# A gather of weight rows in two halves, each with its own signal, in a sparse mixture-of-experts kernel on one core

## What is computed

```python
rates = relu(x) * 0.001
c = cond[:, None, :] + cumsum(rates, axis=1)
spikes = (floor(c) - floor(c one step earlier)) / 0.001      # mostly zero
probs = softmax(spikes @ router_w.T);  top 2, gates normalized to sum 1
keep = position of the token within its expert < C           # C = 640
h = gelu(einsum('ech,ehf->ecf', expert_in, w1))              # w1: 8 x 256 x 1024
y = einsum('ecf,efh->ech', h, w2)                            # w2: 8 x 1024 x 256
out = x + sum over the two experts of gate * y
```

## Time and profile before

| | us |
|---|---|
| median of 3 runs | 68.56 |
| lowest and highest run | 67.09, 68.94 |
| the profiled execution's own time | 67.18 |
| its span, first to last instruction | 65.5 |
| TensorE busy within the span (PE) | 53.0 |
| VectorE (DVE), ScalarE (ACT), GpSimd (POOL) busy | 36.2, 25.9, 18.2 |

### The profile page before, as it was taken

One profiled execution on the slowest core, in us unless ns is written; L12 is line 12 of the kernel. 1 busy time (PEld: TensorE's weight loads), 2 busy tenths in 40 slices (PEclk: granted clock), 3 DMA queues, 4 the chain that ended last, 5 costly groups with the idle time before them and its releaser, 6 DMA issues.

```text
span 65.5 us, 1291 instructions
## 1 busy us (share of the span) xinstructions
PE 53.0 (81%) x435; PEld 32.7 (50%) x435; DVE 36.2 (55%) x165; ACT 25.9 (39%) x60; POOL 18.2 (28%) x55
## 2 busy tenths in 40 slices
PE   3985999999679971199979999999999999994000
PEld 1312434554345661144539668986597666661000
DVE  0377097877799677988668924867061022026000
ACT  0599425756770039409996300681027002000000
POOL 6799943000002500306668810000000000000740
PEclk9999999999999998555599999999999999999985
DMA  0499999999999999700487860698899991000030
GB/s 0 119 362 320 353 329 355 370 336 344 345 349 348 351 350 343 219 13 0 105 190 228 326 234 35 134 357 283 264 381 384 382 358 35 0 0 0 15 126 10
DMA packets 13545, 14.82 MB, mean 226 GB/s; under 512 B 652, under 2 KB 13046, under 8 KB 13536
## 3 DMA queue, kind: packets, MB, share of 16 engines
q1 hardware_dynamic: 12608, 12.62, 59.4%
q0 software_dynamic: 816, 2.01, 9.9%
q10 hardware_dynamic: 112, 0.07, 0.5%
HBM read 13.08 MB, written 2.36 MB: 236 GB/s over the span
## 4 chain that ended last, share of the span: by engine, by line
PE 63%; ACT 8%; DVE 7%; DMA 7%; issue 5%; POOL 3%; ACTq 2%; POOLq 0%; DVEq 0%
PE bank L662 22%; PE bank L646 12%; PE bank L501 11%; DMA w_got<-in_L_ffn_w_dram,w_index 7%; PE bank L552 6%; POOL out_dram L476 3%; ACT w_got L753 3%; PE bank L507 3%; PE bank L518 2%; PE bank L678 2%; ACT L753 2%; ACTq L749 1%; PE bank L567 1%; PE bank L679 1%; ACT limit L790 1%
## 5 line engine op out<-in xcount | busy, mean ns | idle before, releaser
L662 PE MATMUL bank<-w_sb,spare_sb 128*64 128x256 f32 x128 | 14.7, 382 | 0.0
L662 PEld LDWEIGHTS bank<-w_sb,spare_sb 128*64 128x64 f32 x128 | 8.8, 137 | 4.5
L488 PE MATMUL bank<-ones_b 128*128 128x512 bf16 x23 | 9.4, 555 | 1.1 <-POOL ones_b L380 1.1
L501 PE MATMUL bank<-rate,cum_seq 128*128 128x512 f32 x16 | 8.4, 604 | 0.1
L476 POOL DMA_INDIRECT out_dram<-floors,out_index x2 | 2.0, 1020 | 22.9 <-DVE floors L1092 22.6
L646 PE MATMUL bank<-ev_pair,w_got 128*128 128x128 f32 x64 | 7.8, 278 | 0.4 <-DMA w_got<-in_L_ffn_w_dram,w_index 0.4
L770 ACT ACTIVATE spikes<-bank 128x256 bf16<-128x256 f32 x16 | 6.0, 381 | 5.3 <-PE bank L518 5.2
L646 PEld LDWEIGHTS bank<-ev_pair,w_got 128*128 128x128 f32 x64 | 7.4, 192 | 0.9 <-DMA w_got<-in_L_ffn_w_dram,w_index 0.9
L902 DVE TENSOR_SCALAR floors<-bank 128x512 bf16<-128x512 f32 x8 | 5.5, 691 | 3.5 <-PE bank L507 3.2
L783 ACT ACTIVATE spare_sb<-bank 128x512 f32<-128x512 f32 x8 | 4.8, 597 | 6.7 <-PE bank L646 6.6
L996 DVE TENSOR_SCALAR rate<-bank,pair_gate 128x256 f32<-128x256 f32 x4 | 1.9, 484 | 9.2 <-PE bank L662 9.2
(11 more groups left out here) (176 smaller groups left out, 79.2 us busy)
## 6 DMA issues: line engine op xcount, KB each, us to landing
w_sb<-in_L_ffn_w_dram SPq DMA_DIRECT2D x8, 1024.0 KB, 11.3
x_sb<-in_x_dram SPq DMA_DIRECT2D x8, 256.0 KB, 4.1
out_dram<-x_sb SPq DMA_DIRECT2D x1, 2048.0 KB, 13.7
cond<-in_cond_dram ACTq DMA_DIRECT2D x2, 32.0 KB, 2.3
w_got<-in_L_ffn_w_dram,w_index POOLq DMA_INDIRECT x4, 5.8
cond<-in_cond_dram SPq DMA_DIRECT2D x1, 32.0 KB, 1.9
x_rows<-in_x_dram,out_index POOLq DMA_INDIRECT x2, 3.7
out_dram<-floors,out_index POOLq DMA_INDIRECT x2, 2.8
```

What stands on the lines that cost most here:

```text
L488: nc.tensor.matmul(bank[2][:, 0:4 * P], ones_b[:, :], ones_b[:, :].unsqueeze(1).to_broadcast([P, 4, P]), start=True, stop=True)
L501: nc.tensor.matmul(CUM[g % 4][:, 0:GW], cum_seq[:, :], rate[:, g % RING, :, :].rearrange("p j c -> p (j c)"), start=True, stop=False)
L662: mm = nc.tensor.matmul(Y[d % 2][at, :], hT[:, d % 2, f, at], w2_sb[:, 2 * d + side, f, :], start=(f == 0), stop=(f == FC - 1))
```

## The change

`gather(0)` issues two indexed DMAs instead of one: the first loads columns 0 to 511 of each row and raises `w1_in[0]`, the second loads columns 512 to 1023 and raises the new `w1_half`. Both use the same list of rows. `hidden(0)` waits for `w1_in[0]` ahead of half 0 and for `w1_half` ahead of half 1. SyncE, which waits for all of w1 before the last two loads of w2, waits for `w1_half` too. The gathers of the other three groups stay whole, behind the two in GpSimd's queue.

```diff
+        w1_half = sem("w1_half")
...
+        def halves_of(d):
+
+            return ((0, FFN // 2), (FFN // 2, FFN)) if d == 0 else ((0, FFN),)
+
...
                     for d in range(D):
                         sp.wait_ge(w1_in[d], 16)
+                    sp.wait_ge(w1_half, 16)
...
             def gather(d):
                 pool.wait_ge(cleared, d + 1)
                 pool.wait_ge(indexed, d + 1)
-                g.indirect_dma_start(
-                    out=w1_got[:, d, :], out_offset=None, in_=w1_rows[:, :],
-                    in_offset=bass.IndirectOffsetOnAxis(ap=w1_index[:, d:d + 1], axis=0),
-                    bounds_check=E * H - 1, oob_is_err=False, compute_op=ALU.bypass).then_inc(w1_in[d], 16)
+                for part, (lo, hi) in enumerate(halves_of(d)):
+                    g.indirect_dma_start(
+                        out=w1_got[:, d, lo:hi], out_offset=None, in_=w1_rows[:, :],
+                        in_offset=bass.IndirectOffsetOnAxis(ap=w1_index[:, d:d + 1], axis=0), element_offset=lo,
+                        bounds_check=E * H - 1, oob_is_err=False,
+                        compute_op=ALU.bypass).then_inc(w1_half if part else w1_in[d], 16)
...
                 pe.wait_ge(w1_in[d], 16)
                 pe.wait_ge(map_out, d + 1)
                 for half in range(2):
+                    if d == 0 and half == 1:
+                        pe.wait_ge(w1_half, 16)
                     if d >= 2:
                         pe.wait_ge(h_done, 2 * (d - 2) + half + 1)
```

## The result

| us | before | changed |
|---|---|---|
| median of 6 runs each | 68.75 | 69.72 |
| lowest and highest | 67.09, 69.47 | 68.08, 70.22 |
| profiled execution, own time | 67.18 | 69.75 |
| its span | 65.5 | 68.0 |

The ratio is 1.0198, 95% interval 1.0127 to 1.0269: the changed kernel is slower by about 1.3 us (the medians differ by 0.97, the lowest runs by 0.99), where I had forecast +0.06 us. The time itself, 69.72, lies in the forecast range, but above the forecast's own 68.3 to 69.0.

The account below looks back on a forecast made before the run. TensorE was taken to bound the kernel through the end of `hidden(0)`: 0.43 us removed, 0.45 us and rounding added, all else hidden, +0.06 us, so 67.24 against the profiled 67.18, or 68.6 against the median; range 66.8 to 69.9.

Parts of the forecast that it names:

- What bounds the kernel: TensorE, busy 53.0 of 65.5 us; whatever moves the end of `hidden(0)` moves the kernel's end by as much.
- the 0.43 us: TensorE's idle wait ahead of `hidden(0)`, after `keep_warm`: the most that an earlier first half could save.
- The bounds 3.5 and 4.4: Limits in us on the first half's landing after issue: quickest 1 KB-row gather and whole-row gather; 3.8 was taken.
- The second gather on GpSimd: GpSimd's added gather of w1 rows: 0.99 us of its time, starting 0.30 us after the first gather's part.
- The 0.45 us that I gave to the step to gather 1: On GpSimd, the pause between the second half's gather and gather 1, which has a wait: 0.45 us.
- The second half's latency: Second w1 half, issue to landing: 4.1 us forecast, landing at 35.24; break-even against the old kernel at 4.04 us.
- the forecast's 0.45: TensorE's new wait between the two halves of `hidden(0)`, from 34.83 to 35.28: 0.45 us added.
- rival 1: Bytes decide the second half's latency: it lands by 34.8, TensorE's wait vanishes, 66.8 us (68.2 against the median); chance 0.18.
- All else hidden: Later gathers, x_rows, SyncE's w2 loads and the output copy move later but still arrive in time: no added time.
- Rival 3: Gather 1 takes over 7.5 us, so `hidden(1)` waits; 1 us beyond that gives 68.2 us (69.6); chance 0.04.
- 0.15 to slower: Whole kernel: forecast chance 0.15 that the change measures slower; about 2% was taken as what a measurement can tell.
- the 0.79: Whole kernel: forecast chance 0.79 that the measured time stays the same; faster had 0.06.

## Why the prediction was right and wrong

- **What bounds the kernel, and the 0.43 us.** Right. In all fourteen profiles without the lateness the last adds begin 22.98 to 23.02 us behind the end of `hidden(0)`, and `keep_warm` caps the first half: it began right behind these products (33.22) though it had landed 3.4 us after its issue, at 33.1. On chip 1 it took 4.06 us and began at 33.81. The bounds 3.5 and 4.4 were nearly right. But the 0.43 us hung on when the clock rose: it was 0.51 us on chip 15 and nothing in both profiles of the whole gather with 10 products, where the clock rose at 33.69 and 34.49.
- **The second gather on GpSimd.** Right: 1.00 us, 0.30 us behind the first (forecast 0.99 and 0.30). The 0.45 us that I gave to the step to gather 1 was 0.30.
- **The second half's latency.** Forecast 4.1 us, measured 3.49, 3.76 and 3.73 in the three profiles with a visible wait. This is the term of the sum that was mis-sized, by 0.3 to 0.6 us: the rows of before told that 4 KB rows take 4.4 and 1 KB rows 3.5 to 3.8, and 2 KB rows take no more than 1 KB rows. That the gap of 0.38 us came out near the forecast's 0.45 is luck: half 0 too ran 0.6 us earlier than I had it, with the clock up at 31.88, not 32.57. With half 0 at 33.8 as forecast, a landing 3.49 us after 31.14 would have left no gap, which is rival 1. The estimate of 3.82 us by the Trainium skill (DMA: Bandwidth & Descriptors, "Anatomy of one DMA — SWDGE (gpsimd) path") was nearer than mine, and still above all three.
- **"All else hidden".** This is the step that failed. I looked at what is queued behind the added gather on GpSimd and when each is wanted, and that was right: on chip 15 gathers 1 to 3 landed 5.2 to 5.3 us after their issue, as in the kernel before on that chip and sooner than the earlier trace rows has them, and SyncE's loads went out at 40.45, not 41.4. I put it at nothing that the added gather could make other engines' signals late. In the first measurement VectorE's copies of the third and fourth map waited up to 1.97 us, and VectorE, which I had as idle cover, became the engine that TensorE waited for: 0.26 + 0.55 us, and the last adds came 0.81 us later behind the first gather. What makes the signals late stays open. In the earlier trace rows the gathers stand beside the maps in time; the link between them isn't in the trace of before at all. Rival 3, "a later gather is late", named the symptom (`hidden(1)` late, by 0.81 us) with the wrong cause.
- **The time.** The loss of the first measurement has a chip's part. Where the signals are on time the ratio is 1.000, 1.004 and 0.998 (the last with 10 products); where they are late, the changed kernel or a kernel with the same added gather loses 1.0 to 2.0 us, its quickest run against the quickest of before. In the first measurement and on chip 0 the profiles account for 0.81 and 0.71 us of this; the rest is not explained. I gave 0.15 to slower and rested the 0.79 on one chip's record.
- **The scatter.** I used the 1.85 us between runs only for a chance. The place was in the first microseconds of the trace that I had: about 1 us of idle TensorE between the warm-up and the first products, as in the two traces above. It was worth more than the whole change: a median 0.9 to 1.7 us lower on chips 1, 6 and 0. On chip 15, where most runs of the kernel before were quick as it is (median 67.37), two more products were not tried, and there is little to gain.

Of all that ran, the whole gather with 10 warm-up products is the version to keep: 67.8 against 68.73 on chip 1, 67.59 against 69.25 on chip 0 (it ran on these two alone). The split adds nothing measurable to it where the signals are on time, and loses where they aren't.

## To carry to other kernels

Splitting a load pays only what the consumer's engine idles, less what the second load's later issue takes; here, on chip 15, 0.51 us against 0.38, and 0.1 us was left. Where the consumer's engine is busy until the load has landed, it pays nothing. Price an added indexed load not only by its own engine's queue but by what runs beside it, and measure it on more than one chip before believing that it is hidden. When runs of one kernel form two groups, find the first row in which two traces differ before working on anything else.

## What the runs showed of the hardware

- An indexed load of 128 rows of 2 KB landed 3.4 to 4.1 us after its issue, of 4 KB rows 4.1 to 4.4 us when first in the queue, and 4.7 to 4.9 us with another gather 0.3 us behind. GpSimd's own part was 0.98 to 1.11 us for any of these sizes.
- With an added gather in GpSimd's queue, TensorE's signals reached VectorE so late, in the first measurement and on chips 0 and 13, that it waited 1.2 to 2.0 us instead of at most 0.65, and in no profile on chips 15, 1 and 6. The cause is not known, and the recording itself is not ruled out.
- With eight warm-up products and about 1 us of idle time behind them, 2.4 GHz began at 4.06 to 5.26 us in some executions and at 9.55 to 10.40 in others: 0.82 or 1.46 us for the same three products, 1.5 us of the kernel's time. With ten it began by 6.38 in all twelve profiles, and the medians on chips 0, 1 and 6 were 67.5 to 67.95 us for whole rows and for halves, wherever the signals were on time, against 68.7 to 69.3 for the kernel before.
- A stop of 1.21 us in TensorE's work was followed, in one profile, by 3.4 us at 1.2 GHz.
